# A depthwise 5x5 convolution on one Trainium2 core: the first channels' transfers, splits and sums in another order

## The reference, cut to what matters

```python
ch = x.shape[-1]                                   # x: (128, 55, 55, 96) float32
k = jnp.transpose(kernel, (1, 2, 0))[:, :, None, :]
y = lax.conv_general_dilated(x, k, window_strides=(1, 1), padding='SAME',
                             dimension_numbers=('NHWC', 'HWIO', 'NHWC'), feature_group_count=ch)
return x + y
```

## Time and profile before

| what | us |
|---|---|
| median of 3 runs (lowest to highest) | 806.69 (806.47 to 806.73) |
| the profiled execution's own time | 806.57 |
| its span, first to last instruction | 804.8 |
| PE busy | 795.2 (99%) |
| DVE busy | 675.4 (84%) |
| ACT busy | 644.5 (80%) |
| POOL busy | 520.7 (65%) |

### The profile page before, as it was taken

How to read it: one execution, slowest core, us unless ns; L and a number is a source line. 1 busy time by engine, 2 the same in 40 slices (tenths; PEclk the granted TensorE clock), 3 DMA queues, 4 the chain that set the end, 5 groups by cost and what they waited for, 6 DMA issues and landing times.

```text
span 804.8 us, 20077 instructions
## 1 busy us (share of the span) xinstructions
PE 795.2 (99%) x6831; PEld 793.1 (99%) x6831; DVE 675.4 (84%) x2776; ACT 644.5 (80%) x1541; POOL 520.7 (65%) x194
## 2 busy tenths in 40 slices
PE   7999999999999999999999999999999999999997
PEld 7999999999999999999999999999999999999997
DVE  7888888888888888888888888888888888888886
ACT  6778888787878888787878788787878788787875
POOL 2675766667675767666675757666675757666672
PEclk9999999999999999999999999999999999999999
DMA  9999999999999999999999999999999999999975
GB/s 364 418 388 399 399 398 394 397 406 391 394 399 398 395 401 392 399 400 395 398 392 402 394 396 396 396 403 396 393 392 403 388 401 389 405 401 388 397 286 236
DMA packets 32358, 313.41 MB, mean 389 GB/s; under 512 B 3584, under 2 KB 6528, under 8 KB 7936
## 3 DMA queue, kind: packets, MB, share of 16 engines
q1 hardware_dynamic: 31968, 311.67, 97.9%
q10 hardware_dynamic: 288, 0.46, 0.2%
HBM read 161.13 MB, written 150.99 MB: 388 GB/s over the span
## 4 chain that ended last, share of the span: by engine, by line
PE 97%; DMA 1%; DVE 1%; SPq 0%; issue 0%; ACT 0%; DVEq 0%
PE sums L481 82%; PE sums L470 9%; PE sums L468 5%; DMA x_in<-x 1%; SPq L313 0%; DVE x_low L285 0%; DVE y_out L392 0%; DVE y_out L386 0%; ACT x_high L346 0%; DVE y_out L381 0%; DVE taps_split L262 0%; DVE y_out L395 0%; ACT y_out L354 0%; DVE rest L266 0%; DVEq L178 0%
## 5 line engine op out<-in xcount | busy, mean ns | idle before, releaser
L481 PE MATMUL sums<-weights,x_high 121*128 121x226 f32 (+3 forms) x4032 | 689.6, 275 | 0.0
L481 PEld LDWEIGHTS sums<-weights,x_high 121*128 121x128 f32 x4032 | 611.1, 192 | 0.0
L481 PE MATMUL sums<-weights,x_low 121*128 121x226 f32 (+3 forms) x2016 | 546.8, 271 | 1.8 <-DVE y_out L392 1.1
L354 ACT ACTIVATE y_out<-sums 128x242 f32<-128x242 f32 (+5 forms) x1344 | 389.6, 378 | 149.8 <-PE sums L481 149.7
L285 POOL TENSOR_TENSOR x_low<-x_in,x_high 121x1920 fp32r<-121x1920 f32 x95 | 411.5, 4332 | 0.0
L481 PEld LDWEIGHTS sums<-weights,x_low 121*128 121x128 f32 x2016 | 387.0, 192 | 2.3 <-DVE y_out L392 1.3
L346 ACT ACTIVATE x_high<-x_in 121x1920 fp32r<-121x1920 f32 (+1 forms) x195 | 298.0, 1528 | 5.0 <-DMA x_in<-x 4.8
L280 POOL TENSOR_TENSOR weights<-taps_split,start_in 121x450 fp32r<-121x450 f32 x95 | 113.0, 1189 | 271.7 <-DVE x_low L285 220.9
L392 DVE TENSOR_TENSOR y_out<-sums,y_out 128x96 f32<-128x96 f32 (+3 forms) x1056 | 258.3, 245 | 11.6 <-DVE y_out L386 1.3
L386 DVE TENSOR_TENSOR y_out<-sums,y_out 128x44 f32<-128x44 f32 (+2 forms) x864 | 177.1, 205 | 93.8 <-ACT y_out L354 3.7
L285 DVE TENSOR_TENSOR x_low<-x_in,x_high 121x1280 fp32r<-121x1280 f32 (+1 forms) x100 | 146.0, 1463 | 0.5 <-ACT x_high L346 0.5
(11 more groups left out here) (13 smaller groups left out, 5.2 us busy)
## 6 DMA issues: line engine op xcount, KB each, us to landing
x_in<-x SPq DMA_DIRECT2D x95, 1600.0 KB, 12.6
y<-y_out SPq DMA_DIRECT2D x95, 1536.0 KB, 8.5
taps_in<-taps SPq DMA_DIRECT2D x22, 150.0 KB, 12.8
x_in<-x SPq DMA_DIRECT2D x5, 320.0 KB, 6.0
y<-y_out SPq DMA_DIRECT2D x3, 302.5 KB, 2.3
y<-y_out SPq DMA_DIRECT2D x1, 357.5 KB, 3.7
start_in<-start ACTq DMA_DIRECT2D x1, 300.0 KB, 4.9
y<-y_out SPq DMA_DIRECT2D x1, 271.0 KB, 2.4
```

What stands on the lines that cost most here:

```text
L354: act.activation(y, sums, ACT.Copy).then_inc(tile_copied, 1)
L481: product = pe.matmul(sums, v[slot][0:SQUARE, at:at + IMAGES], window, start=n == 0 and v is x_low, stop=n == len(squares) - 1 and part == ...
```

## The change

**Steps of DVE.** For a lone square the step on its own pixels moves between the two column seams, and row seams wait for DVE's earlier steps only where the tile above is a lone square. Column seams wait as before.

**Second channel.** Its input comes in two transfers, as its two pieces (1280 and 1920 columns), each with a semaphore.

**First transfer.** `start_in` holds the taps of channel 0 alone: 375 columns instead of 600. The taps of channels 0 to 3 come as a transfer of their own behind it on ACT's queue.

**Strip one.** In the first piece of channel 0 PE makes all products of the high part of x first, and waits for the low part only ahead of the rest. There are two more products with zeros ahead.

**POOL.** Ahead of `place_taps` of channel 1, POOL no longer waits for DVE's low part.

```diff
-ZERO_PRODUCTS = 15
+ZERO_PRODUCTS = 17
...
-        start_in = sbuf("start_in", [P, (BATCH + 1) * TURNED_COLS + TAP_COLS], F32)
+        start_in = sbuf("start_in", [P, 2 * TURNED_COLS + TAP_COLS], F32)
...
+        second_loaded = sems("second_loaded", len(LATER_PIECES))
...
-            given = given_taps(batch)[:, first:end, :]
+            given = taps_in[batch % TAPS_SLOTS][0:SQUARE, first:end, :]
+            if batch == first == 0:
+                given = start_in[0:SQUARE, 0:TURNED_COLS].unsqueeze(1)
...
             for j in range(GRID):
                 cols = piece_cols(0, j)
                 sp.dma_start(x_in[0][:, cols], x[0, :, cols]).then_inc(first_loaded[j], 16)
-            for c in range(1, X_SLOTS):
+            for piece in range(len(LATER_PIECES)):
+                cols = piece_cols(1, piece)
+                sp.dma_start(x_in[1][:, cols], x[1, :, cols]).then_inc(second_loaded[piece], 16)
+            for c in range(2, X_SLOTS):
                 load_x(c)
...
                     act.wait_ge(first_loaded[piece], 16)
+                elif c == 1:
+                    act.wait_ge(second_loaded[piece], 16)
...
             act.dma_start(start_in[:, :], start).then_inc(start_loaded, 16)
+            load_taps(act, 0)
             load_taps(act, 1)
...
                 dve.wait_ge(tile_copied, copied(c, i))
                 if alone(i):
                     own, low_sums = fresh(c, i, LOW)
+                    if col_seam(i):
+
+                        seam = y_view(c, j - 1)[:, first:end, FRESH[j - 1] - SEAM:FRESH[j - 1]]
+                        dve.wait_ge(y_step, stepped(c, i - 1) - col_seam(i - 1))
+                        dve.tensor_tensor(seam, sums[:, :, 0:SEAM], seam, ALU.add).then_inc(y_step, 1)
                     dve.tensor_tensor(own, low_sums, own, ALU.add).then_inc(y_step, 1)
+                    if col_seam(i):
+                        dve.wait_ge(y_step, stepped(c, i - 1) + 1)
+                        dve.tensor_tensor(seam, sum_view(c, i, LOW)[:, :, 0:SEAM], seam, ALU.add).then_inc(y_step, 1)
+                    return
                 if row_seam(i):
-
-                    dve.wait_ge(y_step, stepped(c, i - 1))
+                    if alone(i - 1):
+
+                        dve.wait_ge(y_step, stepped(c, i - 2) + 1 + col_seam(i) if i > 1 else stepped(c, 0))
...
                     dve.wait_ge(y_step, stepped(c, i - 1))
                     dve.tensor_tensor(seam, sums[:, :, 0:SEAM], seam, ALU.add).then_inc(y_step, 1)
-                    if alone(i):
-                        dve.wait_ge(y_step, stepped(c, i) - 1)
-                        dve.tensor_tensor(seam, sum_view(c, i, LOW)[:, :, 0:SEAM], seam, ALU.add).then_inc(y_step, 1)
...
             for c in range(1, CHANNELS):
-
-                pool.wait_ge(low_by_dve[c % SLOTS], lows(c, 0))
+                if c > 1:
+
+                    pool.wait_ge(low_by_dve[c % SLOTS], lows(c, 0))
                 place_taps(pool, c)
                 split_low(pool, c, 1, low_by_pool)
...
+                by_low, by_high = ((x_low, HIGH),), ((x_high, HIGH), (x_high, LOW))
                 for piece, (first, end) in enumerate(pieces_of(c)):
-
                     low_ready = low_by_dve if by_dve(c, piece) else low_by_pool
+                    tiles = [i for i in range(len(TILES)) if first <= TILES[i][0] < end]
+                    if (c, piece) == (0, 0):
+
+                        pe.wait_ge(high_ready[slot], highs(c, piece))
+                        for i in tiles:
+                            products(c, i, by_high, True, False)
+                        pe.wait_ge(low_ready[slot], lows(c, piece))
+                        for i in tiles:
+                            products(c, i, by_low, False, True)
+                        continue
+
                     pe.wait_ge(low_ready[slot], lows(c, piece))
-                    for i in range(len(TILES)):
-                        if first <= TILES[i][0] < end:
-                            tile(c, i)
+                    for i in tiles:
+                        wait_bank(c, i)
+                        products(c, i, by_low + by_high, True, True)
```

More of the change, by code:

```diff
@@ L442, in wait_bank, with products @@
                     pe.wait_ge(tile_copied, copied(c + back, before))
-            def tile(c, i):
+            def products(c, i, kinds, starts, stops):
                 j, squares = TILES[i]
@@ L447, in tile @@
                 first_col, cols = SUM_COLS[j]
-                wait_bank(c, i)
                 for n, square in enumerate(squares):
@@ L458, in tile @@
                     run = lead + count + (lead + count) % 2
[L459 to L463, removed]
-                        else:
-                            windows = weights[slot][0:SQUARE, :, origin:origin + (end - first) * WINDOW].rearrange(
-                                "p w (r c) -> p w r c", c=WINDOW)[:, :, :, first_col:first_col + cols]
-                            sums = psum[:, bank_of(c, i), 0:2 * run].rearrange("p (w r c) -> p w r c", w=2, c=cols)
-                        pe.matmul(sums[:, HIGH], x_low[slot][0:SQUARE, at:at + IMAGES], windows[:, HIGH],
-                                  start=True, stop=False, skip_group_check=True)
-                        product = pe.matmul(sums, x_high[slot][0:SQUARE, at:at + IMAGES], windows,
-                                            start=False, stop=True, skip_group_check=True)
-                        break
@@ L473, in tile @@
-                    for v, part in ((x_low, HIGH), (x_high, HIGH), (x_high, LOW)):
-                        if cols == WINDOW:
-                            window = weights[slot][0:SQUARE, part, origin - lead:origin - lead + run]
-                            sums = psum[:, bank_of(c, i), to - lead:to - lead + run]
-                        else:
-                            window = weights[slot][0:SQUARE, part, origin:origin + (end - first) * WINDOW].rearrange(
-                                "p (r c) -> p r c", c=WINDOW)[:, :, first_col:first_col + cols]
-                            sums = psum[:, bank_of(c, i), to:to + count].rearrange("p (r c) -> p r c", c=cols)
-                        product = pe.matmul(sums, v[slot][0:SQUARE, at:at + IMAGES], window,
-                                            start=n == 0 and v is x_low,
-                                            stop=n == len(squares) - 1 and part == LOW, skip_group_check=True)
@@ L484, in tile @@
-                product.then_inc(tile_summed, 1)
+                    if cols == WINDOW:
+                        windows = weights[slot][0:SQUARE, :, origin - lead:origin - lead + run]
+                        sums = psum[:, bank_of(c, i), to - lead:to - lead + run]
+                        both = psum[:, bank_of(c, i), 0:2 * run].rearrange("p (w n) -> p w n", w=2)
+                    else:
+                        windows = weights[slot][0:SQUARE, :, origin:origin + (end - first) * WINDOW].rearrange(
+                            "p w (r c) -> p w r c", c=WINDOW)[:, :, :, first_col:first_col + cols]
+                        sums = psum[:, bank_of(c, i), to:to + count].rearrange("p (r c) -> p r c", c=cols)
+                        both = psum[:, bank_of(c, i), 0:2 * run].rearrange("p (w r c) -> p w r c", w=2, c=cols)
@@ new lines, in products @@
+                    for v, part in kinds:
+                        ends = {"start": starts and n == 0 and (v, part) == kinds[0],
+                                "stop": stops and n == len(squares) - 1 and (v, part) == kinds[-1]}
+                        pixels = v[slot][0:SQUARE, at:at + IMAGES]
+                        if alone(i) and part == LOW:
+                            continue
+                        if alone(i) and v is x_high:
+                            ends["stop"] = stops and kinds[-1][0] is x_high
+                            product = pe.matmul(both, pixels, windows, skip_group_check=True, **ends)
+                        else:
+                            product = pe.matmul(sums, pixels, windows[:, part], skip_group_check=True, **ends)
@@ L487, in _ @@
+                if stops:
+                    product.then_inc(tile_summed, 1)
             pe.wait_ge(zeros_ready, 1)
```

19 lines of the change are left out of this document (7 added, 12 removed).

## The result

The changed kernel takes **810.38 us** (median of 6 runs, 809.59 to 810.79) against 806.64 us of the kernel before in the same comparison: a ratio of 1.0047, 95% interval 1.0036 to 1.0057. It is slower by 3.7 us, where 804.6 was forecast, within 803.8 to 806.9. The time lies in the direction of the first rival (809.2), and 1.2 above it.

What follows compares the result with a forecast made beforehand. PE (99% busy) bounds the kernel; only time before its last gap can be won. Tile 8 of channel 1 at 21.48 instead of 23.57 gives 2.1 us: 806.57 to 804.5, median 0.12 above, 804.6; range 803.8 to 806.9.

Steps and rivals of the forecast that it cites:

- Rival 1: POOL gets its turn between two DVE operations, twice; tile 13 waits until 20.8: slower, 809.2 us, chance 0.15.
- Frame: Only time before PE's last gap counts: the result is how much earlier than 23.57 tile 8 of channel 1 starts.
- The start: Smaller first transfer lets DVE begin 0.3 us sooner; PE starts near 7.0, 1.1 sooner; added zero products cost nothing.
- So of the 1.1 us of the early start 0.8 us are lost again here: Tile 8 of channel 0 waits for DVE's step on tile 0, so starts at 12.08 instead of 12.38.
- Piece 0 and piece 1 of channel 1: Earlier landings start ACT's high parts at 11.3 and 13.2, and POOL's low part at 15.1, 2.1 us sooner.
- The 0.25 us for the steps of tiles 0 to 4: DVE's steps ahead of channel 1's piece 0 get 0.25 us shorter through a lost wait and the new order.
- In the forecast DVE keeps its turn: DVE's low parts of strips three to five leave POOL no gap, since the next starts 0.08 us before the last ends.
- PE has no idle time there to take it: In the rest of the run, time DVE gets back from lost waits is worth nothing.
- Rival 2: Only the first turn goes to POOL; tile 8 of channel 1 comes at 22.5: 805.6 us, chance 0.13.
- Rival 3: Channel 1's two transfers land as late as the whole did; only start and steps gain: 806.0 to 806.4, chance 0.12.
- The rest of the sum: POOL's low part at 15.1, DVE's for channel 2 from 18.5 to 20.8, tile 8 of channel 1 at 21.48.

Runs made afterwards that it cites:

- e3: The kernel before, with only POOL's wait for channel 1 taken away: 806.44 us, ratio to before 0.9996.
- e7: e1 with the taps of channels 0 to 3 in the first transfer again (300 KB): 805.15 us.
- e1: The changed kernel with POOL's wait for DVE's low part put back ahead of placing channel 1's taps: 804.57 us.
- e8: e1 with strip one's products in the old order (low part first) and 15 products with zeros: 804.46 us.
- e5: e1 with channel 1's input in one transfer again: 805.72 us.
- e6: e1 with DVE's steps in the old order with the old waits: 805.45 us.
- e9: The changed kernel with POOL's first low part as two operations queued one behind the other (640 and 1280 columns): 806.61 us.
- e2: The changed kernel, POOL still placing channel 1's taps early but waiting for DVE's L257 before its first low part: 804.44 us.
- e4: The changed kernel, POOL placing channel 1's taps after DVE's five low parts and starting its first low part after L257: 803.65 us.

## Why the prediction was wrong, point by point

- **Frame: right.** The result was set by what comes before the last gap, and PE ran without a gap behind it.
- **The start: right in kind, the term too small.** I took 0.3 us for the smaller transfer; DVE began at 4.92 instead of 5.76, 0.84 sooner. Over all profiled executions it began between 4.75 and 5.13 with the small transfer and between 5.76 and 5.99 with the big one (before, e3, e7). In e7 it began at 5.84; the profiled execution of e7 is 0.8 longer than that of e1, its median 0.58. PE's first product started at 7.00 as forecast, but set by the end of the zeros (7.17 for the last) and not by the weights (6.37). The two added products with zeros were priced at 0.34 each and took 1.01 together (7.17 against 6.16). It makes no difference, as e8 shows.
- **"So of the 1.1 us of the early start 0.8 us are lost again here": right in kind, and more was lost.** Tile 8 started at 12.42, not 12.08, since DVE's low parts were stretched by POOL's first turn. Without it (e1) it started at 11.53.
- **Piece 0 and piece 1 of channel 1: right.** ACT's second high part let POOL start its low part at 14.69 (forecast 15.1), and e5 gives 1.15 us for the two transfers. ACT's first high part started at 10.69 (forecast 11.3). The 0.25 us for the steps of tiles 0 to 4 was right too: from DVE's step on tile 0 to its low part are 1.69 in e1 (11.15 to 12.84) and 1.95 in e6 (11.14 to 13.09).
- **"In the forecast DVE keeps its turn, because its next operation starts some 0.08 us before the last has ended": this step failed**, and the result with it. The recorded start of DVE's next operation isn't the moment from which it holds the port. POOL, waiting since 9.18 and 14.69, was next each time, and e9 shows the same the other way round. The rule of the Trainium skill (SBUF — State Buffer, "Who interferes with whom": issue order decides who blocks) was quoted against the forecast, and the trace agrees with it: POOL's start is recorded at 14.69 and L257's at 15.13, and L257 stood; 3.20 for 2.29, and 4.50 for 0.46. It deserved the larger chance: the forecast set an inference from overlapping records against it, which nothing in the trace of before had tested.
- **Rival 1: its mechanism was right.** It had tile 13 at 20.8 (19.96 measured: 0.57 of the 0.84 because DVE's low part for channel 1 started at 13.73 and not at 14.3, the rest because L257 stood for 4.04 and not for 4.3) and 809.2 in all. What it lacked is the clock: 2.72 us at the half clock behind the long gap. What it had too much is 0.84 at tile 13 and the 0.64 of the later channels.
- **"PE has no idle time there to take it, so that is worth nothing": wrong by 0.64 us.** The page shows no idle time in the later channels, but in the kernel before seven products there were longer than the others, by up to 0.1. e6 shows the loss, and the row at 648.32 what it waited for.
- **Rival 2** (one turn only) was e2's case, with 805.6 forecast and 804.44 measured; tile 8 of channel 1 came at 22.10 and not at 22.5, and with the 0.64 of the later channels, which the sum hadn't counted, that is 1.0 of the 1.16 between them. **Rival 3** is out: ACT's first high part of channel 1 ran at 10.69, where it ran at 13.13 before, and back in one transfer (e5) the time rose by 1.15.
- **The rest of the sum: e4 shows it.** There POOL's low part starts at 14.74 (forecast 15.1), and none of DVE's operations ahead of it is stretched, as the forecast had it. DVE's low part of channel 2 took from 17.94 to 20.43 (2.49 with its wait for POOL; forecast 18.5 to 20.8), and tile 8 of channel 1 came at 21.11 (forecast 21.48). In the changed kernel this low part ran only at 23.82, behind POOL's end, and took 1.49. e4's 803.65 is 0.95 under the 804.6: 0.37 by tile 8 and 0.64 by the later channels, less 0.06. So had the failed step held, e4 suggests a time near 803.65, under the forecast and just under its range: besides that step, the sum had POOL's low part 0.36 too late and the later channels at nothing.

## What to carry to other kernels

Before a wait between DVE and GpSimd is removed, list for each operation of GpSimd which DVE operations with two SBUF inputs are queued at the time it will ask, and what stands behind them; a long GpSimd operation that asks just before a short one of DVE costs nearly its whole length (4.04 of 4.34 here). An edit that is harmless alone (the wait, e3) and one that gains alone (the early data, 1.15 us from e5 to e1) can be harmful together, so the times at which the others ask must be worked out again after each edit. Where a long gap of PE is among the outcomes, the half clock behind it belongs in its price.

## What the runs showed of the hardware that I had not expected

- In these runs the port between DVE and GpSimd changed hands at the end of an operation when the other engine waited, even between two operations of one engine whose recorded starts and ends overlap by 0.08 us (L280 3.20 for 2.29, e2 as well) and in both directions (e9: L258 1.81, POOL's pair 5.06). DVE's steps, which read `sums` from PSUM, aren't held: in the kernel before, while POOL's low part ran (17.20 to 21.54), this one took its usual 0.20:

```profile
18.82 0.20 DVE L386 TENSOR_TENSOR y_out<-sums,y_out 128x44 f32<-128x44 f32 x1
```

- PE's granted clock was at 1.2 GHz for 6.8 us, from 1.1 us before the end of a gap of 4.3 us; a gap of 1.6 us was followed by 3.5 us of it in the profiled execution of e9, 1.8 us after products had resumed, and the times and mean clocks of its 11 executions suggest that 7 had it and 4 had not. Gaps of 1.4 and 1.56 us (e2, e5) were followed by none in their profiles.
- Waits of PE of about 0.1 us don't show as idle time. The lengths of the products tell them (up to 0.37 instead of 0.27), and so does the time over many channels.
